# Reordering one step of a software-pipelined RWKV mixing stage: differences, gate product, router logits and the first products of the mix

## The reference

```
x = x + 0.5 * ffn(layernorm(x))
x = x + attn(layernorm(x))
x = x + 0.5 * ffn(layernorm(x))

ffn:  logits = x @ router_w.T + router_b;  top 2 of 16 experts, softmax gates
      place of a token in its expert = number of earlier tokens of that expert
      kept if place < 1280;  out = sum over 2 of gate * (gelu(x @ w1 + b1) @ w2 + b2)

attn: xx  = shift(x) - x                       # shift: one token back
      xxx = x + xx * maa_x
      lora = tanh(xxx @ maa_w1)                # 5 groups of 32
      m_f = lora_f @ maa_w2_f                  # f = w, k, v, r, g
      x_f = x + xx * (maa_f + m_f)
      r, k, v = x_r @ Wr, x_k @ Wk, x_v @ Wv;  g = tanh(x_g @ gw1) @ gw2
      w = exp(-exp(time_decay + tanh(x_w @ dw1) @ dw2))
      y_t = r_t @ (S + u * k_t v_t);  S = w_t * S + k_t v_t     # per head of 64
      out = (groupnorm(y) * ln_g + ln_b) * g @ Wo
```

## Time and profile before

| | |
|---|---|
| time, median of 3 runs | 3143.79 us (3139.49 to 3144.29) |
| profiled execution, its own time | 3144.1 us |
| its span (first to last instruction) | 3142.4 us |
| PE busy over the span | 2773.4 us, 88% |
| DVE / ACT / POOL busy | 2017.5 / 1572.8 / 1256.9 us |
| one step of the mix, all groups present | 54.69 us (1411.08 to 1465.77) |

### The profile page before, as it was taken

How to read it: one execution, slowest core, us unless ns; L and a number is a source line. 1 busy time by engine, 2 the same in 40 slices (tenths; PEclk the granted TensorE clock), 3 DMA queues, 4 the chain that set the end, 5 groups by cost and what they waited for, 6 DMA issues and landing times. The chain is left out here.

```text
span 3142.4 us, 63449 instructions
## 1 busy us (share of the span) xinstructions
PE 2773.4 (88%) x21936; PEld 2236.8 (71%) x21936; DVE 2017.5 (64%) x4620; ACT 1572.8 (50%) x2733; POOL 1256.9 (40%) x1072
## 2 busy tenths in 40 slices
PE   6354999999999995899899999974899999999997
PEld 6343888888888882566566666653788888888886
DVE  5354665666666653688888888863566666666664
ACT  5232665656665652344444444421556656656653
POOL 2652332222322223456676666644122322223233
PEclk9999999999999997999999999966899999999998
DMA  9924454544545527101111111001644545545444
GB/s 344 310 74 107 87 95 80 89 87 86 88 80 88 94 28 260 50 21 39 41 43 36 49 36 43 31 30 46 125 87 86 92 78 89 90 85 87 79 75 146
DMA packets 540964, 281.26 MB, mean 90 GB/s; under 512 B 397591, under 2 KB 503131, under 8 KB 540480
## 3 DMA queue, kind: packets, MB, share of 16 engines
q1 hardware_dynamic: 478624, 202.67, 25.8%
q0 software_dynamic: 57888, 75.16, 14.0%
q10 hardware_dynamic: 4224, 0.52, 0.1%
HBM read 150.83 MB, written 146.41 MB: 95 GB/s over the span
## 5 line engine op out<-in xcount | busy, mean ns | idle before, releaser
L763 POOL DMA_INDIRECT acc_a<-ae_ob,ae_to x160 | 260.2, 1626 | 675.7 <-ACT ae_ob L712 623.2
L763 POOL DMA_INDIRECT acc_b<-be_ob,be_to x150 | 243.5, 1623 | 636.3 <-ACT be_ob L712 534.0
L730 ACT ACTIVATE be_h<-be_pH,b 128x512 f32<-128x512 f32 (+1 forms) x384 | 236.8, 617 | 359.8 <-PE be_pH L657 334.4
L730 ACT ACTIVATE ae_h<-ae_pH,b 128x512 f32<-128x512 f32 (+1 forms) x384 | 236.8, 617 | 344.8 <-PE ae_pH L657 327.6
L1464 POOL TENSOR_TENSOR m_xf<-m_tmp,m_xT 128x512 f32<-128x512 f32 x160 | 181.3, 1160 | 150.6 <-DVE m_tmp L1179 150.5
L1757 PEld LDWEIGHTS m_PP<-m_RP,m_KS 64*64 64x64 f32 x6656 | 124.2, 142 | 106.9 <-issue 105.8
L1757 PE MATMUL m_PP<-m_RP,m_KS 64*64 64x64 f32 x6656 | 139.4, 229 | 56.3 <-DVE m_A L1208 49.4
L1515 POOL DMA_INDIRECT slots_b<-m_row,m_sidx x128 | 137.7, 1076 | 117.7 <-issue 117.7
L464 POOL DMA_INDIRECT slots_a<-ar_row,ar_sidx x128 | 125.8, 982 | 130.8 <-issue 105.9
L1179 DVE SCALAR_TENSOR_TENSOR m_tmp<-m_B,m_ch,m_xx 128x512 f32<-128x512 f32 x160 | 111.9, 741 | 71.3 <-PE m_B L1847 37.9
L657 PE MATMUL ae_pH<-ae_xT0h,ae_w_0h 128*128 128x512 f32 (+1 forms) x256 | 88.1, 344 | 53.8 <-DVE ae_xT0l L839 51.4
(11 more groups left out here) (343 smaller groups left out, 9009.5 us busy)
## 6 DMA issues: line engine op xcount, KB each, us to landing
ae_stage<-in_w SPq DMA_DIRECT2D x64, 512.0 KB, 3.5
be_stage<-in_w SPq DMA_DIRECT2D x64, 512.0 KB, 3.6
slots_a<-empty SPq DMA_DIRECT2D x5, 4160.0 KB, 25.0
slots_b<-empty SPq DMA_DIRECT2D x5, 4160.0 KB, 31.5
ae_xq<-slots_a SPq DMA_DIRECT2D x252, 64.0 KB
be_xq<-slots_b SPq DMA_DIRECT2D x252, 64.0 KB
ar_xin<-in_x SPq DMA_DIRECT2D x16, 512.0 KB, 10.1
m_xin<-acc_a SPq DMA_DIRECT2D x16, 512.0 KB, 4.8
```

Of the source, the lines that this page charges most:

```text
L730: t = act.activation(dst[:, 0:SIZES[b]], pH[c % 2][:, 0:SIZES[b]], ACT.Gelu, bias=S.b1[:, bass.ds(i * (2 * FC) + (u * FC + f), 1)])
L763: pool.indirect_dma_start(S.acc[tag][:, :], bass.IndirectOffsetOnAxis(ap=to[m][:, q:q + 1], axis=0), ob[m][:, q, :], None, bounds_check=T ...
```

## The change

Instructions of every engine are put in another order. `m_xx` becomes two buffers, so the differences of X no longer wait for the last mixes of F. `m_xxx` loses its own buffer and lies over `m_wl`, so `differences` waits until ACT has made the decays of F from `m_wl` (`w_ready`), and `clamp` waits until `low_rest` has read `xxx`. No arithmetic changes.

```diff
@@ buffers
-        xx = sb("xx", [P, DC, GT])
-        xxx = sb("xxx", [P, DC, GT])
+        xx = [sb(f"xx{u}", [P, DC, GT]) for u in range(2)]
+        xxx = wl[:, :].rearrange("p (c t) -> p c t", c=DC)
@@ order of PSUM fills: ("C", s - 2, b) now behind ("O0", s - 1, a)
@@ DVE, differences(g)
-                    drained(dve, "M9", g - 1)
...
                     filled(dve, "LG", g - 1)
+                    hold(dve, w_ready, g)
@@ DVE, clamp(g, k)
+                    filled(dve, "LG", g)
@@ DVE, one step
                     keep(L, 4)
+                    if live(X):
+                        differences(X)
                     if live(F):
                         for m in range(8, 10):
                             mix_in(F, m)
-                    if live(X):
-                        differences(X)
                     if live(K):
                         spread(K)
                     factors(L, 4)
                     keep(L, 5)
-                    if live(R):
-                        choose(R)
                     factors(L, 5)
                     keep(L, 6)
                     if live(K):
                         gated(K)
-                    factors(L, 6)
                     if live(R):
-                        places(R)
+                        choose(R)
                     if live(X):
                         for m in range(2):
                             mix_in(X, m)
+                    factors(L, 6)
                     if live(K):
                         add_out(K, 0)
+                    if live(R):
+                        places(R)
@@ POOL, one step
-                        scatter(Z, (0, 1))
+                        scatter(Z, (0,))
+                    if live(K):
+                        gate(K)
                     if live(F):
                         for m in range(8, 10):
                             mix_add(F, m)
                     if live(K):
-                        gate(K)
                         root_spread(K)
                     if live(Z):
-                        scatter(Z, (2, 3))
+                        scatter(Z, (1, 2, 3))
@@ ACT, one step: untie(ROUTE, R) now ahead of keys(F); shares(R) now last
@@ PE, one step
-                    if live(L):
-                        level(L, 2)
                     if live(F):
                         rate(F, 0)
                     if live(L):
+                        level(L, 2)
+                    if live(L):
                         gates(L, 0)
+                    if live(R):
+                        turn_route(R)
                     if live(F):
                         project(F, "K", Wk, 1)
-                    if live(R):
-                        turn_route(R)
...
                     if live(F):
-                        mixes_of_rest(F)
+                        mixes_of_rest(F, 0)
                     if live(R):
                         logits(R)
+                    if live(F):
+                        mixes_of_rest(F, 1)
...
-                    if live(R):
-                        prefix(R)
                     if live(L):
                         level(L, 7)
                     if live(X):
                         low_rest(X)
-                    if live(K):
-                        turn_out(K)
                     if live(X):
                         mixes_of(X, range(0, 2))
                     if live(K):
+                        turn_out(K)
                         output(K, 0)
+                    if live(R):
+                        prefix(R)
```

More of the change, by code:

```diff
@@ L1164, in differences @@
                     untied(dve, IN, g)
[L1165 removed]
                     x = xT[g % 2]
[L1167 removed]
+                    d = xx[g % 2]
+                    c(dve.tensor_tensor(d[:, :, :], x[:, :, 0:GT], x[:, :, 1:GT + 1], ALU.subtract))
                     c.settle()
                     filled(dve, "LG", g - 1)
+                    hold(dve, w_ready, g)
                     for k in range(DC):
[L1171 removed]
+                        dve.scalar_tensor_tensor(out=xxx[:, k, :], in0=d[:, k, :], scalar=ch[:, 0, k:k + 1],
                                                  in1=x[:, k, 1:GT + 1], op0=ALU.mult,
```

40 lines of the change are left out of this document (19 added, 21 removed).

## The result

The kernel after takes 3279.77 us (median of 4 runs, 3277.99 to 3282.44) beside 3143.00 us of the kernel before on the same chip (3139.49 to 3144.29): ratio 1.0438, 95% interval 1.042 to 1.0456. The forecast was 3166 with a range to 3184. The direction was right, the size was off by a factor of six: +137 us instead of +22.

What follows compares the result with a forecast made beforehand. PE and DVE both nearly full; the chain through both sets the step. Steps 3 to 13 +21 us, steps 1 and 2 +6, drain -5: +22 on 3144.1, so 3166 us, own range 3153 to 3182, overall 3112 to 3184.

Steps and rivals of the forecast that it cites:

- Level 2: Product of the decay's first half moved into PE's 0.59 us wait ahead of level 2: gain 0.4 us, bounds 0 and 0.59.
- Differences ahead of M8 and M9: DVE makes the differences while waiting for M8; the gate product gets between the two `xxx`; V starts at 31.6 instead of 29.24.
- Rival B: POOL doesn't get between the two `xxx`: V at 29.3, 2.4 us less a step, 3113 us (3137 with low clock); chance 0.24.
- Level 5 to level 6: Level 5 at 35.2, DVE in time, PE's 2.38 us wait gone; level 6 stays at 40.10.
- Level 6 to level 7: `choose` (3.30 us on DVE) leaves this place; level 7 comes 3.3 us behind level 6 instead of 5.15, gain 1.85.
- Level 7 to the next step: Prefix, ACT's copy and handover, and a wait for `places` add 1.8 us (1.0 to 2.6): 11.2 instead of 9.44.
- rival C: The end of the step is 1 to 2 us worse, or the clock falls there too: 3190 us; chance 0.09.
- The clock: PE's idle stretch ahead of V lowers its clock, now paid in full from V to level 6: 2.0 us a step (0 to 3.4).
- Rival A: No clock loss, all else as forecast: 3140 us; chance 0.16.
- Steps 0 to 2: Only steps 1 and 2 were counted: V's later start and longer end about 1 us, clock 2, together 6 us (2 to 9).
- Step 14 and the drain: In the drain `choose` and the gate product come off the path two or three times: 5 us less (0 to 9).
- the forecast's sum (+1.9): Net change per step for steps 3 to 13: -0.1 without the clock loss plus 2.0 for it; times 11 is 21 us.

Runs made afterwards that it cites:

- b_diff_early: Kernel before with only DVE's differences moved ahead of the last two mixes, with the two buffers of xx and their waits; 3144 chip: ratio 1.0134.
- a_r_first: Kernel after with level 5 moved behind the R product on PE; 3082 chip: ratio 1.0408, and 1.0392 when run again.

## Why the forecast was wrong, point by point

*Level 2, gain 0.4: not there.* Level 4 starts at 23.09, before 22.95, and the front added to b_diff_early gave nothing. The product that was moved had run beside another, step 3 before and after:

```profile
1421.11 0.69 PE L1887 MATMUL m_B<-m_twg,m_dgw 64*128 64x512 f32 x1
1421.11 0.70 PE L1906 MATMUL m_B<-m_dgw,m_twg 64*128 64x256 f32 x2
...
1439.00 1.12 PE L1890 MATMUL m_B<-m_twg,m_dgw 64*128 64x512 f32 x2
1441.15 1.13 PE L1909 MATMUL m_B<-m_dgw,m_twg 64*128 64x256 f32 x4
```

Before, the two took 1.06 us together (1421.11 to the start of the K product at 1422.17); apart, they take 1.12 and 1.13. So the move fills a hole of 0.59 with a product of 1.12 and saves nothing behind level 2. (The forecast's list of PE's idle places also leaves out one of 0.32 us, ahead of L1887 at 1428.15.)

*Differences ahead of M8 and M9: right.* Forecast: the gate product between the two `xxx`, V at 31.6. Measured: V at 32.0 on the mean, the gate product between the two `xxx` in every full step. Rival B (POOL doesn't get between) never happened. The Trainium skill (SBUF — State Buffer, "Who interferes with whom") has such a pair exclude each other for a whole instruction; the pair of `xxx` took 3.75 us around a gate product of 2.35, so the trace agrees. (The forecast also called the trace a witness for `mix_in`, which reads PSUM. In the earlier trace rows no arithmetic of POOL runs beside it. In the kernel after it does: the pair at 1492.97 takes 1.40 us with POOL's addition beside it from 1493.79.)

*Level 5 to level 6: this is the step that failed.* The forecast said "Level 5 is at 35.2, level 6 at 40.1: DVE is in time now". DVE was in time, free from 1464.9 on, and did not get level 5. The forecast weighs the indirect DMAs only where they stand ahead of the gate product; the row of six has no term in its sum, and it didn't ask over which work of others that row now stands. The row cost 5.0 us a step against the forecast (9.91 instead of 4.9), 55 us in eleven steps and 2 to 5 more in step 14 (61.73 against 56.45 and 59.60 in the two kernels without the six). Taking the DMAs away or spacing them gave this back: 3204 and 3220 us instead of 3280. It is not the whole miss: without the row a step is 58.48 us and the forecast's is 56.6. There level 5 to 6 is 4.79 and level 6 to 7 3.30, both as forecast, and what is left is the tail, 13.16 us instead of 11.2. A sign of the row's wait was in the rows of before: the 0.94 us of PE waiting for its own halves, inside a row of four. I read it as a gap to be filled, and took the difference of 5.46 us as POOL's doing alone.

*Level 6 to level 7: mechanism right.* With the clock full it is 3.3, as forecast (3.29 in steps 4, 11 and 13 of the kernel after); on the mean 4.17, since level 6 and `low` run at the low clock behind the long wait in the other steps (1.99 and 2.51 us in step 3, granted clock 0.66).

*Level 7 to the next step: undersized.* Forecast 11.2, measured 12.07, and 12.6 to 13.2 where the row is spaced or gone. The wait ahead of the first output product is there (1.18, forecast 1.1). The second is 1.23 in step 3 and 1.04 on the mean instead of 0.4: `places` ends at 62.3 of step 3. DVE's two factors ahead of it take 1.15 and 1.57 us instead of 0.65 each, in the same time as the copies of ACT to `m_Af` and POOL's additions. On the 3082 chips, where no row holds anything, the tail is 12.82 instead of 9.69: it costs 3.1, where leaving the place ahead of level 7 gives 1.6. A part of rival C was true.

*The clock: right in size.* Taken as 2.0 a step. V lasts 6.12 us on the mean instead of 3.69 at full clock, so 2.4, behind idle stretches of 2.2 to 3.2; in no full step is it under 5.1, and the granted clock over it is 0.54 to 0.72. Rival A is out.

*Steps 0 to 2: +16.6, where steps 1 and 2 were to cost 6.* They cost 10.1, and step 0, which the forecast left out, 6.5. "V's later start about 1 us" was 2.6 to 3.2 (level 4 to V: 3.93, 5.45, 5.45 before; 6.51, 8.59, 8.60 after): in these steps the base had no late halves, so more of the differences' length counts. *Step 14 and the drain: +12 instead of -5.* Step 14 has the row's wait too. What the drain behind it lost 5.4 us by was not looked into.

On the 3082 chips the failed step doesn't exist, and the change is still 3.2% slower: level 4 to V +3.45, V +1.9, level 5 to 6 -0.8, level 6 to 7 -1.6, the tail +3.1, sum +6.35 us a step with +0.3 for level 4. So the forecast's sum (+1.9) was too small there by other errors: V's delay was counted against a base that the late halves had already delayed by 1.0; the 2.3 us that were to be won from level 5 to level 6 were mostly the stalled `m_xx`, which the base does not have there, and only 0.8 came; and the tail.

What stays open: why PE's semaphores are updated late on some chips while POOL issues indirect DMAs, and what differs between the chips. The profile shows it from outside only. Nor is every signal late: the second half of V ended at 1469.14, 1.0 us into the row, and ACT copied it at 1469.18. In the stalled stretch no instruction fetch starts or ends with the wait: the instruction queues moved one block at 33.3 and the next at 49.1 of the step at 1624.55, around a wait that ended at 45.7. Whether a level is more exposed than a large product was to be told by a_r_first, which ran on a chip without the wait.

## What to carry to other kernels

When indirect DMAs issued by POOL are moved, ask which handovers between other engines the row now covers, and above all whether a level that others wait for runs in it; a short pause between the DMAs (here 1.3 us instead of 0.3) is a cheap test. A small unexplained wait of an engine for its own work, as the 0.94 us here, is worth a question before it is used as free room. Two chips can disagree on the sign of such a remedy (the pauses gave about 60 us on one and cost 17 on another), so an order that is tuned to a few tenths of a microsecond is tuned to a chip.

## What the runs showed of the hardware that was not expected

- On the 3144 chips, PE's results reached DVE, ACT and PE itself late while POOL issued indirect DMAs 0.3 us apart: up to 7.6 us in the kernel after, to 1.1 us behind the row's last DMA (8.6 us from the row's start; in the version with rows of four 5.9). It was the update of PE's semaphore that came late (level 5: 1476.69 for products that ended at 1472.55). PE's own stream of 64x64 products ran on for 46 to 52 of 64 and then in pieces of 1 to 6 with idle stretches of mostly 0.38 us between. With pauses of 1.3 us there was almost none of it (factors 4 at 1.67 on the mean instead of 1.23 behind level 5). On the 3082 chips it was not there at all.
- The kernel before takes 3144 and 3082 us on the two kinds, and steps without indirect DMAs last the same on both (52.63 and 52.64).
- A loss of clock that was free in the kernel before (V at 5.9 instead of 3.7 us) went with the longer kind of step once the row had moved: where the kernel before had a row of six, the four steps with V in 5.8 to 6.0 us took 61.5 to 64.1 us, the seven with V in 3.7 to 5.4 us 54.9 to 60.9.
- Two products of 64 rows, L1887 and L1906, ran beside each other and took 1.06 us together; apart they took 1.12 and 1.13.
